# A gated cross-attention layer with routed experts: four row buffers, earlier W_qv loads, a split gather and a split last tile

## Chip, cores and metric

The kernel runs on one core of a Trainium2 chip. The metric is the device time of one execution in microseconds, median of several runs. Engines are called by their profile names: PE (TensorE matmul), PEld (its weight loads), DVE (VectorE), ACT (ScalarE), POOL (GpSimd), SP (SyncE, which here only issues DMAs).

## What is computed

Inputs are x (4096 x 512), a context of 3202 x 512, and the weights. Cut to what matters, the reference is:

```
# attention: queries = LN(x) = e, context = c
Sim  = (e @ w1)[:, None] + (c @ w2)[None, :] + (e * w3) @ c.T + b
hq   = softmax(Sim, axis=1) @ c
hc   = softmax(max(Sim, axis=1)) @ e                  # one row of 512
x    = x + tanh(g_x) * (concat[e, hq, e*hq, e*hc] @ W_qv + b_qv)     # W_qv: 2048 x 512
# routed feed-forward: 8 experts, top 2, CAP = 1.25 * 4096 / 8 = 640 rows each
xf   = LN(x); gates = softmax(xf @ w_router + b_router); top-2, kept while an expert has room
out  = gelu(rows_e @ w1[e] + b1[e]) @ w2[e] + b2[e]   # 512 -> 2048 -> 512 for each expert
x    = x + tanh(g_f) * (weighted sum of the kept outputs, divided by the kept weights' sum)
```

## The kernel before, in words

All matrix products are made of float16 pairs: an operand is split into a high and a low half, and three matmuls (high x high, high x low, low x high) add up in PSUM. One SBUF tensor, `arena`, is cut by hand into tiles for three stages which follow each other; each engine runs its own program and all order between them is by semaphores written out by hand.

**Attention** (`attention`) goes over 16 blocks of 256 rows, two units of 128 rows each, with the context in seven chunks of 512 (the last of 130). Each half of its loop does the scores of unit u on PE (line 1217), the exponentials of u-1 on ACT and DVE (lines 1048 to 1064 and 771), their transposes by DMA from SP (line 530) and the products of u-2 on PE (line 1233). Features (e, hq, e*hq as float16 pairs) go to DRAM (`store_f`, line 544). In the last two halves (`last=True`) no scores are left; SP loads the four parts of W_qv there (`load_weights`, line 266), ACT sums |W| part by part (`sum_part`, 276), POOL reduces over partitions (288), DVE makes the scales (297 to 309) and folds hc into the first part (`fold_part`, 339). Behind both halves ACT and DVE make the twelve high and low halves (`high` 359, `low` 373), and PE merges block 0 (`merge`, 367) once its features are back, transposed (`load_feats`, 249).

**Merge and routing** (`merge_and_route`) has blocks b = 0 to 15 of 256 rows. PE: 72 matmuls of 512 columns (line 1719, two row tiles q of twelve steps of three), and between them the counts of block b-2 (1752), the transposes of the rows of b-1 (1727) and the router of b-1 (1740). DVE, body b: second half of the routing of b-2 (`route_2`, 1513 to 1540), bias and matmul result added (1458, 1460), first half of the routing of b-1 (`route_1`, 1488 to 1504), the other row tile, then the norm (1468 to 1476) and the low halves (1480). ACT: copies of the transposed rows, the routing's exponential (1660), the square root (1662), the high halves (1667). The rows lie in `row[v]`, v = b % 2, a third one serving for the last block; POOL scatters them to the experts' lists in DRAM by four indirect DMAs per block (1426), waits until they have landed and then increments `row_free[v]` (1441), for which ACT and DVE of block b+2 wait. The first expert's w1 is prepared on the side: maxima on DVE (159) in blocks 6 to 9, scales behind 10, split by ACT and DVE (196, 202) in blocks 11 to 14. The last block goes row tile by row tile (`rows_last`, `norm_last`, `lows_last`, `route_1_last`, `route_2_last`).

**Experts** (`experts`), e = 0 to 7: rows of the expert gathered transposed (`turn_rows`, 1858, two DMAs of 320 rows), layer 1 in 16 feature tiles, each for two halves of 320 rows (2012), Gelu on ACT (1976), split on ACT and DVE (1979, 1935); layer 2 in five tiles of 128 rows (2027), whose result DVE scales and biases (1946), ACT weights (1992) and POOL adds to the output by an indirect DMA (1891).

Of the kernel before, what the change touches and what calls it, by code (L numbers as in the profile page):

```python
# [31 lines left out]
P = 128  # L32
# [174 lines left out]
class MergeOperands:  # L207
# [4 lines left out]
    def __init__(self, nc, st, arena, at, NB, w_qv, b_qv, g_x, g_f, w_r, b_r, hc):  # L212
# [12 lines left out]
        for v in range(2):  # L225
            self.ft[v] = take([3, 2, KD, 256], F16)
            self.x2[v] = take([2, D], F32)
            if v == 0:
                self.scores = off[0]
        self.end = off[0]  # L230
        take, _ = cutter(arena[:, at:])
# [32 lines left out]
    def load_weights(self, eng, n):  # L264
        part = slice(n * self.KD, (n + 1) * self.KD)
        eng.dma_start(self.W[:, part, :], self.w_qv.rearrange("(c p) d -> p c d", p=P)[:, part, :])\
           .then_inc(self.w_loaded[n], 16)

    def sum_part(self, act, n):
# [3 lines left out]
        if n:  # L273
# [3 lines left out]
                       self.W.rearrange("p c d -> p (c d)")[:, n * size:(n + 1) * size], ACT.Abs,  # L277
# [12 lines left out]
    def scales(self, dve):  # L290
# [4 lines left out]
        s.n = self.steps  # L295

# [29 lines left out]
    def fold_hc(self, dve):  # L326

        s = Steps(dve, self.prep, 0, 40)
        s.link(dve.reciprocal(self.rw, self.hc["wtot"]))
# [3 lines left out]
    def fold_part(self, dve, k):  # L333
# [5 lines left out]
        s.step(dve.scalar_tensor_tensor(out=self.W[:, k, :], in0=self.W[:, 3 * self.KD + k, :],  # L339
                                        scalar=self.hcn[:, k:k + 1], in1=self.W[:, k, :], op0=ALU.mult,  # L340
                                        op1=ALU.add))
        self.steps = s.n
# [14 lines left out]
    def high(self, act, k, ready):  # L357
        act.wait_ge(self.prep, ready)
        act.mul(self.Wt[:, k, 0, :], self.W[:, k, :], self.sc3[:, k // self.KD:k // self.KD + 1]).then_inc(self.w_hi, 1)

    def merge(self, pe, q, out):

        pe.wait_ge(self.f_loaded[0], 16)
        for k in range(self.FT):
            pe.wait_ge(self.w_lo, k + 1)
            for s, r in ((0, 0), (0, 1), (1, 0)):
                mm = pe.matmul(out[:, q, :], self.ft[0][:, k // self.KD, s, k % self.KD, q * P:(q + 1) * P],  # L367
                               self.Wt[:, k, r, :], start=(k + s + r == 0), stop=(k == self.FT - 1 and s == 1))
        mm.then_inc(self.y_done, 1)

    def low(self, dve, k):
        dve.wait_ge(self.w_hi, k + 1)
        dve.scalar_tensor_tensor(out=self.Wt[:, k, 1, :], in0=self.W[:, k, :],
# [4 lines left out]
def attention(nc, st, ps, arena, cst, x, ctx, w_sim, b_sim, feats, rows, hc_out, mg):  # L378
# [27 lines left out]
    qT = take([QT, 2 * KD, P], F16)  # L406
    qh = take([QT, 2, D], F16)
# [80 lines left out]
    COPIES = (0, 32, 64)  # L488
    UNIT0 = FIRST[0][LAST] + 1

# [6 lines left out]
    def sync(sp):  # L497
# [53 lines left out]
        def body(b, first=False, last=False, norms=True, loads=True, piece=None):  # L551
            u = 2 * b
            for c in range(NC):
# [14 lines left out]
                if c == 4 and not first:  # L568
                    store_f(u - 3, 1)
# [1548 lines left out]
```

## Time and profile before

| | |
|---|---|
| median of 3 runs (lowest, highest) | 2236.64 us (2236.12, 2238.46) |
| the profiled execution | 2254.05 us |
| its span, first to last instruction | 2252.3 us |
| PE busy | 96% of the span |
| DVE, ACT, POOL busy | 58%, 51%, 6% |
| mean granted clock of TensorE | 0.989 |

The shares are means over three stages with different limits, so they are read stage by stage: the timeline of an engine, the chain of waits, and the table of who waited for whom. Starts are in microseconds from the first instruction. Matmuls are pipelined: a row of the timeline ends about 0.16 us after the next one's start, so periods are taken from start to start.

### The profile page before, as it was taken

How to read it: one execution, taken by the hardware profiler on the slowest of the kernel's cores; microseconds unless marked ns; L12 is line 12 of the kernel's file. 1: busy time of each engine (PE TensorE's matmuls, PEld its weight loads, DVE VectorE, ACT ScalarE, POOL GpSimd, SP SyncE). 2: the span in 40 equal slices, each digit the busy share in tenths (PEclk: the TensorE clock that was granted, in tenths of full speed). 3: DMA queues.
4: the chain of work that ended last, by engine and by line, in shares of the span. 5: the costliest groups of instructions: out<-in, count | busy, mean ns of one | idle time of the engine just before them, and what ended most of it. 6: DMA issues, size and time to landing. Idle time of an engine off the chain costs nothing.

```text
span 2252.3 us, 34528 instructions
## 1 busy us (share of the span) xinstructions
PE 2172.4 (96%) x12015; PEld 1123.7 (50%) x12015; DVE 1301.3 (58%) x2712; ACT 1142.2 (51%) x1747; POOL 145.7 (6%) x141
## 2 busy tenths in 40 slices
PE   5999999999999999999999995999999999999997
PEld 2444444444444444444455442646565565647463
DVE  7756566655555665554667665555556464646450
ACT  6765565655555655655433342625354363636260
POOL 0000000000000000000022222010101010010101
PEclk9999999999999999999999997999999999999999
DMA  9534444444444444335987762353433333343511
GB/s 250 133 86 94 111 110 104 106 111 93 92 108 109 111 97 115 87 84 120 269 232 206 186 160 50 144 128 100 103 102 98 107 93 107 93 116 117 132 35 23
DMA packets 484566, 265.91 MB, mean 118 GB/s; under 512 B 423860, under 2 KB 423988, under 8 KB 480428
## 3 DMA queue, kind: packets, MB, share of 16 engines
q1 hardware_dynamic: 473644, 244.90, 41.6%
q0 software_dynamic: 10880, 20.52, 4.8%
q8 instruction: 18, 0.29, 0.1%
q14 instruction: 24, 0.20, 0.0%
HBM read 97.96 MB, written 71.52 MB: 75 GB/s over the span
## 4 chain that ended last, share of the span: by engine, by line
PE 88%; DMA 4%; DVE 4%; issue 2%; ACT 1%; POOL 1%; SPq 0%; POOLq 0%; DVEq 0%; ACTq 0%
PE ps L1217 23%; PE ps L1233 22%; PE ps L2012 19%; PE ps L2027 18%; PE ps L1719 5%; DMA rows<-arena 2%; PE ps L367 1%; POOL rows L1426 1%; DMA arena<-arena 1%; DMA arena<-in_ctx 1%; DVE arena L202 0%; DMA feats<-arena 0%; DVE arena L742 0%; DMA arena<-feats 0%; ACT arena L1667 0%
## 5 line engine op out<-in xcount | busy, mean ns | idle before, releaser
L1217 PE MATMUL ps<-arena 128*128 128x512 f16 (+1 forms) x2688 | 557.0, 358 | 4.8 <-DMA arena<-arena 3.1
L1233 PE MATMUL ps<-arena 128*128 128x512 f16 x2400 | 552.9, 379 | 0.0
L2012 PE MATMUL ps<-arena 128*128 128x320 f16 x3072 | 421.1, 300 | 12.2 <-DMA arena<-rows 12.2
L2027 PE MATMUL ps<-arena 128*128 128x512 f16 x1920 | 415.7, 379 | 0.0
L1217 PEld LDWEIGHTS ps<-arena 128*128 128x128 f16 x2688 | 250.1, 98 | 285.5 <-issue 4.9
L1233 PEld LDWEIGHTS ps<-arena 128*128 128x128 f16 x2400 | 233.6, 98 | 275.7
L2012 PEld LDWEIGHTS ps<-arena 128*128 128x128 f16 x3072 | 301.5, 98 | 131.5 <-DMA arena<-rows 12.2
L1038 ACT ACTIVATE arena<-ps,arena 128x512 f32<-128x512 f32 (+1 forms) x224 | 163.4, 731 | 389.6 <-PE ps L1217 389.5
L2027 PEld LDWEIGHTS ps<-arena 128*128 128x128 f16 x1920 | 187.9, 98 | 225.2
L758 DVE TENSOR_REDUCE arena<-arena 128x1 f32<-128x512 f32 (+1 forms) x224 | 139.9, 626 | 192.5 <-ACT arena L1038 191.7
L771 DVE SCALAR_TENSOR_TENSOR arena<-arena 128x512 f16<-128x512 f32 x192 | 144.1, 751 | 182.4 <-ACT arena L1059 182.4
L1719 PE MATMUL ps<-arena 128*128 128x512 f16 x1080 | 240.9, 380 | 0.0
L1935 DVE SCALAR_TENSOR_TENSOR arena<-arena 128x640 f16<-128x640 f32 x128 | 113.0, 883 | 133.9 <-ACT arena L1979 133.9
L196 ACT ACTIVATE arena<-arena 128x1024 f16<-128x1024 f32 x128 | 140.8, 1134 | 70.5 <-DVE arena L178 70.5
L202 DVE SCALAR_TENSOR_TENSOR arena<-arena 128x1024 f16<-128x1024 f32 x128 | 160.3, 1282 | 16.0 <-ACT arena L196 16.0
L1976 ACT ACTIVATE arena<-ps,arena 128x640 f32<-128x640 f32 x128 | 113.2, 885 | 107.6 <-PE ps L2012 107.5
L1059 ACT ACTIVATE arena<-arena 128x512 f16<-128x512 f32 x192 | 156.1, 813 | 21.4 <-DMA arena<-arena 8.2
L1719 PEld LDWEIGHTS ps<-arena 128*128 128x128 f16 x1080 | 103.0, 98 | 117.5 <-issue 1.8
L1946 DVE SCALAR_TENSOR_TENSOR arena<-ps,arena 128x512 f32<-128x512 f32 x40 | 30.0, 751 | 226.6 <-PE ps L2027 226.6
L1992 ACT ACTIVATE arena<-arena 128x512 f32<-128x512 f32 x40 | 28.8, 719 | 254.8 <-DVE arena L1946 252.9
L159 DVE TENSOR_REDUCE arena<-arena 128x1 f32<-128x2048 f32 x64 | 144.7, 2278 | 12.8 <-DMA arena<-in_L_ffn_w 12.8
L1048 ACT ACTIVATE arena<-arena 128x512 f32<-128x512 f32 (+1 forms) x224 | 149.1, 666 | 2.5 <-DVE arena L764 1.1
(245 smaller groups left out, 1380.3 us busy)
## 6 DMA issues: line engine op xcount, KB each, us to landing
arena<-in_L_ffn_w SPq DMA_DIRECT2D x64, 1024.0 KB, 10.2
feats<-arena SPq DMA_DIRECT2D x48, 512.0 KB, 2.8
arena<-in_x SPq DMA_DIRECT2D x32, 512.0 KB, 3.6
rows<-arena SPq DMA_DIRECT2D x13, 774.0 KB, 3.7
out<-arena SPq DMA_DIRECT2D x16, 512.0 KB, 3.0
arena<-in_ctx SPq DMA_DIRECT2D x6, 1024.0 KB, 13.4
arena<-arena SPq DMA_TRANSPOSE x276, 3.1
arena<-in_L_xattn_W_qv SPq DMA_DIRECT2D x4, 1024.0 KB, 7.9
```

The source lines that it names most:

```text
L159: s.step(dve.tensor_reduce(self.mw4[:, c:c + 1], self.raw[:, c * n:(c + 1) * n], AX.X, ALU.max, apply_absolute_value=True))
L196: act.mul(w[:, 0, c * n:(c + 1) * n], self.raw[:, c * n:(c + 1) * n], sc[:, 0:1]).then_inc(self.s_hi, 1)
L202: dve.scalar_tensor_tensor(out=w[:, 1, c * n:(c + 1) * n], in0=self.raw[:, c * n:(c + 1) * n], scalar=sc[:, 0:1], in1=w[:, 0, c * n:(c + 1 ...
L771: dve.scalar_tensor_tensor(out=stage[:, c % 2, 1, :], in0=p, scalar=pscale[:, c:c + 1], in1=stage[:, c % 2, 0, :], op0=ALU.mult, op1=ALU.s ...
L1038: act.activation(slot(par, c), psS[bank][:, 0:w], ACT.Identity, bias=zero[:, 0:1], scale=sinv[:, c:c + 1]).then_inc(scores_ready, 1)
L1048: act.activation(p, p, ACT.Exp, bias=neg[:, par:par + 1], accum_out=ls[:, par, c:c + 1])\
L1059: act.activation(stage[:, c % 2, 0, :], p, ACT.Identity, bias=zero[:, 0:1], scale=pscale[:, c:c + 1])\
L1217: mm = pe.matmul(out, qT[:, q, s * KD + k, :], ctxT[:, r * KD + k, a:z], start=(k == 0 and s + r == 0), stop=(k == KD - 1 and s == 1))
L1233: mm = pe.matmul(psO[q], turned, ctxN[:, j, r, :], start=(j + s + r == 0), stop=False)
L1719: mm = pe.matmul(psY[v][:, q, :], ft[v][:, k // KD, s, k % KD, q * P:(q + 1) * P], Wt[:, k, r, :], start=(k + s + r == 0), stop=(k == FT - ...
L2012: mm = pe.matmul(psH[:, f % 2, h, :], w1s[:, s, k * F + f * P:k * F + (f + 1) * P], XT[:, r, k, h * HALF:(h + 1) * HALF], start=(k + s + r ...
L2027: mm = pe.matmul(psO[:, t % 2, :], hT[:, f, s, t * P:(t + 1) * P], w2s[:, r, f * D:(f + 1) * D], start=(f + s + r == 0), stop=(f == KF - 1 ...
```

## The change

Four things are changed.

1. *W_qv and the features of block 0.* W is four tiles; the first two lie where the queries were and are loaded in the second half before the last two (`load_early`), the other two in the places of the first two loads. ACT sums them in chunks 0, 1, 4 and 5 of the half before last. The features of block 0 are requested in that half too (`load_first`). The twelve steps are taken in the order 4 to 11, 0 to 3, and the first five low halves are made before the fold.
2. *Merge and routing.* Four row buffers, b % 4; ACT and DVE wait for the scatter of b-4 directly, POOL for that of b-2, and `row_free` goes. The bias is added at the start of a body, bn_stats follows each row tile, and ACT makes the high half from x2 with scale and bias, no longer from DVE's normalised rows. The w1 maxima move to blocks 4 to 7, the scales behind 8, the split to 9 to 12. DVE, ACT and POOL run without loops. In the last block ACT's exponential of row tile 0 comes ahead of the square root of row tile 1.
3. *Experts.* Four gathers per expert: for each half of the rows first the high, then the low halves, with their own semaphores; layer 1 takes all matmuls of high rows first.
4. *The last tile of the last expert* is made in two halves of 256 columns, in other PSUM banks. ACT weights the bias beforehand, DVE makes the output in one operation per half, and POOL adds each half by a DMA of its own.

```diff
-        self.W = take([4 * KD, D], F32)
+        late = take([2 * KD, D], F32)
+        early = take([2 * KD, D], F32)
+        self.W = [early[:, 0:KD, :], early[:, KD:2 * KD, :], late[:, 0:KD, :], late[:, KD:2 * KD, :]]
+        self.ORDER = tuple(range(KD, FT)) + tuple(range(KD))
...
+        def load_early(n):
+            if n == 0:
+                for q in range(QT):
+                    sp.wait_ge(q_turned[q], 16 * (NB - 1))
+                sp.wait_ge(row_step, RK * U)
+                sp.wait_ge(e_out, 16 * NB)
+            mg.load_weights(sp, n)
...
-                if last and 1 <= c < 5:
+                if last and c in (1, 2):
                     if c == 1:
                         sp.wait_ge(qk_done, NC * U)
-                    mg.load_weights(sp, c - 1)
+                    mg.load_weights(sp, c + 1)
...
+                if last and c == 4:
+                    load_first()
...
+                if last and i and c == 1:
+                    mg.scales(dve)
+                    for n in range(AHEAD):
+                        mg.low(dve, n)
...
-                if last and not i and c >= 4:
-                    mg.sum_part(act, c - 4)
-                if last and i and c == 0:
-                    mg.sum_part(act, 3)
+                if last and not i and c in (0, 1, 4, 5):
+                    mg.sum_part(act, c if c < 2 else c - 2)
...
-    row = [take([QT, ROW], F32) for _ in range(3)]
+    row = [take([QT, ROW], F32) for _ in range(NR)]
...
+        for b in range(NB - 1):
+            pool.wait_ge(r_step, RK * (b + 1))
+            if b >= 2:
+                pool.wait_ge(sent[(b - 2) % NR], earlier(b - 2) + 16 * 2 * QT)
             for q in range(QT):
-                scatter(v, q, v)
+                scatter(b % NR, q)
+            if b == SCALED - 3:
+                ew.reduce_max(pool, 0)
...
             dve.wait_ge(y_done, QT * b + q + 1)
-            s.step(dve.scalar_tensor_tensor(out=x2[v][:, q, :], in0=(psY_first if first else psY[v])[:, q, :], scalar=cY[:, 0:1],
+            s.link(dve.scalar_tensor_tensor(out=x2[v][:, q, :], in0=(psY_first if first else psY[v])[:, q, :], scalar=cY[:, 0:1],
                                             in1=x2[v][:, q, :], op0=ALU.mult, op1=ALU.add))
+            s.step(dve.bn_stats(stats[:, q, :], x2[v][:, q, :]))
...
+            s.step(dve.scalar_tensor_tensor(out=shift, in0=mv[:, :, 0], scalar=-1.0, in1=rs, op0=ALU.mult, op1=ALU.mult))
...
+            if b >= NR:
+                act.wait_ge(sent[r], earlier(b))
+            act.wait_ge(y_step, YK * b + YN + 2)
+            for q in range(QT):
+                act.activation(halves[r][:, q, 0:D], x2[v][:, q, :], ACT.Identity, bias=shift[:, q:q + 1],
+                               scale=rs[:, q:q + 1]).then_inc(hi_done, 1)
...
+        for q in range(QT):
+            copy_turned(NB - 2, q)
+        sd_last(0)
+        exp_of(NB - 2)
+        high_last(0)
+        copy_turned(NB - 1, 0)
+        exp_last(0)
+        sd_last(1)
+        high_last(1)
+        copy_turned(NB - 1, 1)
+        exp_last(1)
...
             for h in range(2):
-                sp.dma_start_transpose(XT.rearrange("p s k c -> p (s k) c")[:, :, h * HALF:(h + 1) * HALF],
-                                       rows[bass.ds(e * CAP + h * HALF, HALF), 0:D].bitcast(F16))\
-                    .then_inc(xt_loaded[h], 16)
+                for r in range(2):
+                    sp.dma_start_transpose(XT[:, r, :, h * HALF:(h + 1) * HALF],
+                                           rows[bass.ds(e * CAP + h * HALF, HALF), r * D // 2:(r + 1) * D // 2].bitcast(F16))\
+                        .then_inc(xt_loaded[h][r], 16)
...
-                    for k in range(KD):
-                        for s, r in ((0, 0), (0, 1), (1, 0)):
+                    for s, r in ((0, 0), (1, 0), (0, 1)):
+                        if f == 0 and s == 0:
+                            pe.wait_ge(xt_loaded[h][r], 16 * (e + 1))
+                        for k in range(KD):
...
+        for c in range(2):
+            cols = slice(c * D // 2, (c + 1) * D // 2)
+            dve.wait_ge(o_done, ST * E + c)
+            dve.scalar_tensor_tensor(out=oa[TL % 2][:, cols], in0=psL[:, c, :], scalar=ali[:, TL:TL + 1],
+                                     in1=o32[TL % 2][:, cols], op0=ALU.mult, op1=ALU.add).then_inc(o_scaled, 1)
```

## Rows read from the trace of the kernel before

**Rows 1.** Busy time per engine in a stretch of merge blocks; PEclk, DMA share, GB/s last

```profile
1190.00:1225.00 35.00, 35.00 (x233) 17.54 (x232) 25.80 (x104) 13.69 (x18) 7.79 (x8) 1.00 0.72 205
```

**Rows 2.** The chain of waits in order of time: start, us, what

```profile
1259.33 9.09 DMA rows<-arena
...
1398.91 5.06 DMA arena<-rows
...
1510.65 52.16 PE ps L2012 x384
```

**Rows 3.** Who waited for whom, 1225 to 1362: total us, times, longest

```profile
ACT arena L1667 <- POOLq L1441: 29.5, 7, 7.3
...
PE ps L1727 <- DVE arena L1480: 8.2, 4, 3.7
```

**Rows 4.** Timeline of PE: start, us, engine, line, operation, count, [idle before]

```profile
1087.11 17.39 PE L367 MATMUL ps<-arena 128*128 128x512 f16 x72 [2.88 <-DMA arena<-feats]
...
1219.51 0.75 PE L1740 MATMUL ps<-arena 128*128 128x8 f16 x24
...
1244.97 0.17 PE L1752 MATMUL ps<-arena 128*128 128x16 f16 x1
...
1262.06 0.17 PE L1752 MATMUL ps<-arena 128*128 128x16 f16 x1
...
1357.54 0.17 PE L1752 MATMUL ps<-arena 128*128 128x16 f16 x1
```

**Rows 5.** Timeline of DVE and ACT behind the last merge matmul of a block

```profile
1225.37 0.75 DVE L1460 SCALAR_TENSOR_TENSOR arena<-ps,arena 128x512 f32<-128x512 f32 x1 [0.50 <-PE ps L1719]
...
1229.04 1.14 ACT L1667 CAST arena<-arena 128x512 f16<-128x512 f32 x2 [0.87 <-DVE arena L1476]
1229.69 1.29 DVE L1480 TENSOR_TENSOR arena<-arena 128x512 f16<-128x512 f32 x2 [0.28 <-ACT arena L1667]
```

**Rows 6.** Line 1059, ACT with scale and bias: ns min/median/max

```profile
L1059 ACT ACTIVATE arena<-arena x192: 812/812/816, 64.9 to 1069.4; 128x512 f16<-128x512 f32 x192
```

**Rows 7.** Timeline of DVE and ACT in the last block, 1362 to 1395

```profile
1363.18 2.48 DVE L202 SCALAR_TENSOR_TENSOR arena<-arena 128x1024 f16<-128x1024 f32 x2 [0.28 <-ACT arena L196]
...
1366.78 0.16 DVE L1513 TENSOR_REDUCE arena<-arena 128x2 f32<-128x16 f32 x1
...
1370.03 0.75 DVE L1575 SCALAR_TENSOR_TENSOR arena<-ps,arena 128x512 f32<-128x512 f32 x1
...
1373.70 0.15 DVE L1585 RECIPROCAL arena<-arena 128x1 f32<-128x1 f32 x1
...
1376.65 0.17 DVE L1513 TENSOR_REDUCE arena<-arena 128x2 f32<-128x16 f32 x1 [0.84 <-ACT arena L1689]
...
1383.73 0.17 DVE L1585 RECIPROCAL arena<-arena 128x1 f32<-128x1 f32 x1 [0.36 <-ACT arena L1675]
...
1385.33 1.28 ACT L1682 ACT_TABLE_LOAD   x1
...
1386.86 0.16 DVE L1513 TENSOR_REDUCE arena<-arena 128x1 f32<-128x8 f32 x1 [0.83 <-ACT arena L1682]
...
1394.34 0.22 DVE L1540 SCALAR_TENSOR_TENSOR arena<-arena 128x2 f32<-128x2 f32 x1
```

**Rows 8.** Timeline of all engines at the end of attention

```profile
1077.17 1.91 ACT L276 ACTIVATE arena<-arena 128x2048 f16<-128x2048 f32 x1 [1.61 <-DMA arena<-in_L_xattn_W_qv]
...
1078.57 6.35 SPq L249 DMA_TRANSPOSE arena<-feats  x1
...
1083.89 8.07 DVE L373 SCALAR_TENSOR_TENSOR arena<-arena 128x512 f16<-128x512 f32 x12 [0.79 <-ACT arena L359]
```

**Rows 9.** Line 530, probability transposes of 128 x 1024 float16, from issue

```profile
DMA to landing us min/median/max: 3.0/3.0/7.6
```

**Rows 10.** Timeline of all engines behind the last matmul, which ends at 2238.38

```profile
2238.48 0.75 DVE L1946 SCALAR_TENSOR_TENSOR arena<-ps,arena 128x512 f32<-128x512 f32 x1 [9.61 <-PE ps L2027]
...
2240.86 1.54 POOL L1891 DMA_INDIRECT out<-arena  x1 [8.81 <-ACT arena L1992]
```

More of the change, by code:

```diff
@@ L869, in half @@
                         total_weight()
-                    if c == 6:
+                    if c == 2:
                         mg.max_router(dve)
-                if last and i and c == 3:
-                    mg.scales(dve)
             if not (last and i):
@@ L989, in vector @@
             half(NB, i, last=True, norms=False)
-        for k in range(FT):
-            mg.low(dve, k)
+        for n in range(AHEAD, FT):
+            mg.low(dve, n)
         mg.router_scale(dve)
@@ L1172, in scalar @@
             half(NB, i, last=True, norms=False)
-        for k in range(FT):
-            mg.high(act, k, mg.scaled)
-            if k == 2:
+        for n in range(FT):
+            mg.high(act, n)
+            if n == 2:
                 mg.gates(act)
@@ L1345, in merge_and_route @@
     pk, kp, tot, away = (take([2, QT], F32) for _ in range(4))
-    dsti = [take([2, QT], U32) for _ in range(3)]
+    dsti = [take([2, QT], U32) for _ in range(NR)]
     wk, wsum, wi = take([QT, 2], F32), take([QT], F32), take([QT], F32)
@@ L1449, in gpsimd, with add_bias @@
         for q in range(QT):
             pool.wait_ge(r_step, RB + RQ * (q + 1))
-            scatter(2, q, 1)
+            scatter((NB - 1) % NR, q)
     def vector(dve):
+        def add_bias(b, v, q):
+            s = Steps(dve, y_step, b, YK)
+            s.n = q
+            s.step(dve.tensor_tensor(x2[v][:, q, :], x2[v][:, q, :], bqb, ALU.add))
         def y_part(b, v, q, first=False):
             s = Steps(dve, y_step, b, YK)
-            s.n = 2 * q
-            s.link(dve.tensor_tensor(x2[v][:, q, :], x2[v][:, q, :], bqb, ALU.add))
+            s.n = YQ[q] - 1
+            s.wait()
@@ L1464, in norm_part @@
+        def norm_part(b, v):
+            r = b % NR
             s = Steps(dve, y_step, b, YK)
-            s.n = 2 * QT
+            s.n = QT + 2 * QT
             s.wait()
-            for q in range(QT):
-                s.step(dve.bn_stats(stats[:, q, :], x2[v][:, q, :]))
-            s.wait()
-            apart(dve, dve_passed)
             for q in range(QT):
@@ L1864, in load_b2 @@
                 .then_inc(b2_loaded, 16)
[L1866 to L1867 removed]
+        for r in sent:
+            sp.wait_ge(r, 16 * rows_sent)
         turn_rows(0)
@@ L1887, in add_rows @@
         def add_rows(e, more=True):
-            for t in range(ST):
+            for t in range(ST if more else TL):
                 pool.wait_ge(o_scaled, ST * e + t + 1)
@@ L1938, in layer_2 @@
         def layer_2(e, more=True):
-            for t in range(ST):
+            for t in range(ST if more else TL):
                 n = e * ST + t
@@ L1983, in layer_2 @@
         def layer_2(e, more=True):
-            for t in range(ST):
+            for t in range(ST if more else TL):
                 n = e * ST + t
@@ L2030, in layer_2, with last_tile @@
                 mm.then_inc(o_done, 1)
-        with pe.Fori(0, E) as e:
+        def last_tile():
+            t = ST - 1
+            for c in range(2):
+                cols = slice(c * D // 2, (c + 1) * D // 2)
+                for f in range(KF):
+                    for s, r in ((0, 0), (0, 1), (1, 0)):
+                        mm = pe.matmul(psL[:, c, :], hT[:, f, s, t * P:(t + 1) * P],
+                                       w2s[:, r, f * D + cols.start:f * D + cols.stop],
+                                       start=(f + s + r == 0), stop=(f == KF - 1 and s == 1))
+                mm.then_inc(o_done, 1)
+        with pe.Fori(0, E - 1) as e:
             layer_1(e)
-            layer_2(e)
+            layer_2(e, ST)
+        layer_1(E - 1)
+        layer_2(E - 1, ST - 1)
+        last_tile()
     return sync, gpsimd, vector, scalar, tensor
```

360 lines of the change are left out of this document (173 added, 187 removed).

## The prediction

> **What bounds the kernel now.** I read the page first: TensorE (PE) is busy 96% of the span, so nearly every microsecond is a matmul slot, and only the places where PE stands can give time back. The chain of waits says where: attention runs PE-bound to 1084, the merge stage is PE-bound until about 1262, then the chain leaves PE, goes through the row scatters and VectorE (DVE), and returns to PE at 1404.0 for the experts, whose steady part has no gap [rows 2]. PE's own timeline gives the sizes. One merge block takes 17.09 us (1244.97 to 1262.06, same instruction), and the five blocks after it take 95.48 [rows 4]. Five periods, less 0.65 because the last block does its count one three-matmul step earlier, are 84.8: **10.7 us** are lost there. The table of waits names the holder: ScalarE's (ACT) high halves of the rows waited 29.5 us in 7 times for the POOL queue's line 1441, which frees a row buffer once its scatter has landed, and PE's transposes then waited for the low halves [rows 3]. One such scatter alone took 9.09 us [rows 2].
>
> **Part 1, four row buffers and the shorter row chain.** Block b now reuses the buffer of b-4, not of b-2, so the awaited scatter has two more periods, 34 us, against 9.09. What is late next? DVE. Its chain after the last merge matmul of a block runs from 1225.37 to the end of the low halves at 1230.98, 5.6 us [rows 5]; PE wants the rows 6.5 us after its block ends. The new chain has one bn_stats of 0.65 fewer behind the matmul, and ACT makes the high half beside the normalising DVE operation. That form of ACT operation (scale and bias per partition) costs 0.81 instead of 0.62 [rows 5, 6], so the chain comes to about 4.9. DVE's order over one block, each from the end of the previous merge: rows 4.9, then in the four blocks with w1 splitting until the second low part, 7.8 (two ACT pieces, two DVE pieces of 1.24 [rows 7]), two bias adds 9.2, second routing half 3.25 [rows 7] 12.4, first half row 13.9, first routing half 15.9. The matmul it waits for next ends at 17.09, so 1.2 us are left; in blocks with a maximum (2.28) more is left. In 35 us of such blocks DVE is busy 25.8 [rows 1]. Added DVE work is one tiny shift operation per block. Block 14 has two more bias adds (1.3) but no split behind it. I take all **10.7** back; bounds 6 (1.2 us late in each of four blocks) and 10.7. The loops written out and the removed semaphore increments I put at nothing, covered by the same slack.
>
> **Part 2, the end of the routing.** Count from T0, PE's start of the last block. Before, T0 is 1354.3 (the count at 1357.54, less five steps of 0.65) and DVE ends at 1394.56: 40.3 us [rows 4, 7]. It spent 12.5 us on rows that waited for a buffer, the last w1 split (2.48) and bias adds, before the routing of block 13 at 1366.78. New: rows until 4.9; routing of 13 until 8.1; wait for PE's first half (8.67: twelve steps of 0.65 and 0.9 of transposes) to 8.8; first half row 1.80, first routing of 14 1.9 (together 1370.03 to 1373.70 plus 0.05): 12.4. Normalise and low: 1.9, to 14.4. The exponential is ready by 12.4, so routing of 14 starts at once; before, it waited until 1376.65. From there to 1383.73 DVE ran without a hole, 7.1 us: 21.5. Normalise and low of the second half 1.85 (it was 3.13 up to 1386.86, where DVE waited for ACT's exponential behind a table load; that exponential is now ahead): 23.3. Then 7.7 as before (1386.86 to 1394.56): 31.1. PE is nearly ahead everywhere; its merge ends at 17.8, its last transposes and ACT's copy at 26.0, before DVE wants them at 26.3. Gain 40.3 - 31.1 = **9.2**; bounds 7 (an ACT table load lands on the chain, and PE is late once) and 10.
>
> A table load took 1.28 us here, and DVE had the activation's result 0.25 us behind its end [rows 7]; it starts ahead of the operands. The Trainium skill ("ScalarE: Activation LUTs", What ACT_TABLE_LOAD costs) speaks against this order: it gives 1.28 us plus a drain of 1.38, so 2.66 per switch. The new order puts the exponential's load ahead of the first high half; by that price the high half would be about 0.9 us late, and the part would give 8.3.
>
> **Part 3, the change of stage at 1084.** Before, PE stood 2.88 us for the feature transposes and ran a half-rate stretch, 17.39 us for 72 matmuls that take 15.55 at 216 ns [rows 4]. The transposes now start in the last attention half, so they are there. What is late next are the scaled weights. The last sum of |W| ended at 1079.2 because the fourth load landed at 1077.1 [rows 8]. With two loads already made a half earlier, the loads of the third and fourth part take the places of the first two, and ACT's order (two sums of 2.1 before the third probability chunk, two after the fifth and sixth) puts the last sum at about 1074.7, two chunks' transposes permitting; reduction 2.1, DVE's output row until 1078.6, scales 1.65: the first high half at 1080.3 instead of 1083.14. Twelve lows took 8.07, so 0.67 each [rows 8]: five until 1084.4. Then, new between them, DVE does totals, four folds and two output lows, 4.9: 1089.3; seven more lows end at 1094.0, and PE's first merge half ends one step later, 1094.7. Before it ended at 1087.11 + 17.39 - 7.77 (36 matmuls) = 1096.7. Gain **2.0**. Against: SyncE's queue (SP) issues the feature transposes in 6.35 us [rows 8], now ahead of the last two probability transposes of the last unit, and PE behind them. They would land at 1081.5 to 1083, where PE wants them at 1080.6 and 1083.2; up to 2.4 us of PE, mostly swallowed since DVE's lows are later. Bounds -1 (that, and a half-rate stretch again) and +4 (no DVE delay). The two early weight loads, one half before, compete with probability transposes that PE needs only a unit later: nothing.
>
> **Part 4, the first expert.** From the issue of the gather to PE's first matmul pass 5.06 us [rows 2]. That DMA moves 655 KB; the probability transposes of 262 KB land in 3.0 [rows 9]. A line through both gives 3.35 for a half of 327 KB: **1.7** earlier; the others follow at about 1.4 each while PE at half rate needs 2.1 us for each eight matmuls. Bounds 0 and 2.1. The other seven experts' gathers lie under layer 2 (240 matmuls of 216 ns, 51.8 us) and cost nothing. The Trainium skill ("DMA: Bandwidth & Descriptors", Anatomy of one DMA) has a fixed 2.0 us plus bytes / 436 GB/s, for the other kind of queue, and so speaks against halving; the rows' fixed part is about 1.6. By its figures a half would take 2.75, and the part would give 2.3.
>
> The new order of matmuls in layer 1 I put at nothing. All pitches here are columns / 2.4 GHz plus 2.5 ns: 52.16 us for 384 of 320 columns [rows 2]. Loads of weights hide even behind 8-column matmuls, 24 of which pass in 0.75 us [rows 4].
>
> **Part 5, the last tile.** Now DVE (0.75), ACT and an issue gap, then POOL's 1.54 at 2240.86 [rows 10]. New: one DVE operation of 256 columns, an estimated 0.50 (0.75 for 512 columns, 1.24 for 1024), and no ACT: 2.48 us from matmul to POOL become 1.45, a gain of 1.03. 96 matmuls of 256 columns take 109 ns each against 48 of 216: 0.1 lost. The first half's add is issued while the second is computed. Landing at the same 5 us: **0.9**; bounds 0 and 1.6 (half the bytes).
>
> **Sum:** 10.7 + 9.2 + 2.0 + 1.7 + 0.9 = 24.5. The profiled execution, 2254.05 (span 2252.3 and 1.75 around it), would become 2229.6. It is 17.4 above the median of the unprofiled runs, 2236.64; I carry the same gain over: **2212.1**.
>
> **Rivals.** (a) *DVE takes the scatter's place*: the 1.2 us of slack is not there, blocks with splits take about 18.2, and the tail keeps a late start: 10.7 becomes 6 and 9.2 becomes 7.5, time 2218.5. For: DVE's link-by-link waits; against: [rows 1]. Chance 0.18. (b) *The change of stage costs instead of gives*: PE waits for the last probability transposes behind the feature transposes and starts at half rate; part 3 is -1 to -2 and the time 2215.5. Chance 0.12. (c) *The profile itself swells the scatter*: without it the landings are shorter and half of the 10.7, and part of the late start, wasn't there to win: gain 16 to 18, time 2219.5. Chance 0.09. (d) *The buffers don't do what they say*: POOL now waits for the scatter of b-2 itself, and if that holds the sends, the rows come as late as before; 10.7 and some 3 of part 2 stay, time 2226. Against: that scatter has a full period. Chance 0.03. (e) *Slower*: layer 1 used each stationary tile twice in a row (high and low rows against the high weights); now never. If the second load of the same tile was free, each of 3072 matmuls pays; from 8 ns each (24.5 / 3072) the change loses, at 12 ns the time is 2249. Against: the router's 24 matmuls of 8 columns change their tile 16 times and take 31 ns each at most [rows 4], so a changed tile finds room beside 320 columns (133 ns). Chance 0.04; about 0.01 of it lies within 0.2% (some 7 to 9 ns).
>
> **How the numbers follow.** Forecast 0.54. Above, the range takes in rivals (a) to (c); below, parts 2 to 5 at their better ends give 2208, and 2 more are for the 17.4 us between profiled and unprofiled runs, which I can't place: 2206 to 2222. Some 0.2% (4.5 us) is what a measurement can tell from no change; only (e) reaches there. Faster 0.96, same 0.01, slower 0.03.
>
> **What would show it.** Merge blocks at 17.09 us without a hole until the last; no ACT wait for a buffer; from T0 to the last routing operation 31 us; the first merge half ending 2 us earlier; 3.4 us from the gather's issue to the first expert matmul; expert periods unchanged at 103.96; POOL's last issue 1.45 after the last matmul. Wrong would make it: PE waiting on DVE lows in blocks 9 to 13, layer 1 over 52.2 us, or a hole in the attention's last unit of more than 3 us.

## The result, and the profile after

The changed kernel takes **2230.61 us** (2229.95 to 2231.76, 8 runs), the kernel before in the same place 2237.84 us (2236.12 to 2241.26, 8 runs): ratio 0.9968, 95% interval 0.9959 to 0.9977. It is faster, by 7.2 us and not by 24.5: the forecast of 2212.1 and its range of 2206 to 2222 missed.

The profiled execution of the changed kernel took 2231.16 us (span 2229.4, clock 0.993). The prediction had 2229.6 for it, so the step from profiled to profiled execution came out within 1.6 us; the step from there to the median did not.

The timeline of PE in the changed kernel; columns as in [rows 4]:

```profile
1064.27 0.49 PE L1272 MATMUL ps<-identf,arena 128*128 128x128 f32 x2 [1.34 <-DVE arena L828]
1084.15 3.41 PE L1255 MATMUL ps<-arena 128*128 128x512 f16 x15 [1.96 <-DMA arena<-arena]
...
1124.59 0.17 PE L1766 MATMUL ps<-arena 128*128 128x16 f16 x1
...
1329.63 0.17 PE L1766 MATMUL ps<-arena 128*128 128x16 f16 x1
1346.07 0.17 PE L1766 MATMUL ps<-arena 128*128 128x16 f16 x1
...
1381.75 3.38 PE L2050 MATMUL ps<-arena 128*128 128x320 f16 x12 [10.55 <-DMA arena<-rows]
1385.46 11.94 PE L2050 MATMUL ps<-arena 128*128 128x320 f16 x84 [0.33 <-DMA arena<-rows]
1398.49 11.72 PE L2050 MATMUL ps<-arena 128*128 128x320 f16 x85 [1.09 <-ACT arena L2012]
```

Line 1766 is the count that was line 1752. Its first start is 1124.59, its thirteenth 1329.63: twelve periods of 17.09 us, and no row with a wait in brackets stands at the transposes of the rows between them. The fourteenth, at 1346.07, stands one step of three matmuls earlier in its block. In the old kernel's trace the same count stood at 1357.54 [rows 4].

DVE, SP and POOL at the end of the routing and of the kernel, and ACT's exponential ahead of the first high half of the last block, from the same timeline:

```profile
1353.86 1.28 ACT L1674 ACT_TABLE_LOAD   x1
1355.15 0.22 ACT L1674 ACTIVATE arena<-arena 128x20 f32<-128x20 f32 x1
1355.76 0.81 ACT L1702 ACTIVATE arena<-arena 128x512 f16<-128x512 f32 x1 [0.39 <-DVE arena L1606]
...
1373.69 0.22 DVE L1566 SCALAR_TENSOR_TENSOR arena<-arena 128x2 f32<-128x2 f32 x1
...
1378.27 6.12 SPq L1873 DMA_TRANSPOSE arena<-rows  x4
...
2217.46 0.48 DVE L2000 SCALAR_TENSOR_TENSOR arena<-ps,arena 128x256 f32<-128x256 f32 x1 [4.66 <-PE ps L2077]
2218.75 1.54 POOL L1923 DMA_INDIRECT out<-arena  x1 [2.25 <-DVE arena L2000]
```

These marks cut the kernel into five stretches, one for each part of the change. C1 and C14 are the first and the fourteenth count, R the end of DVE's last routing operation, Z the start of DVE's last operation on a matmul result, just behind the last matmul. All in us; "predicted" is the gain forecast for that stretch. The parts are numbered 1 to 5 as in the prediction, here and below: the last tile is part 5.

| stretch | before, profile | after, profile | gain | predicted |
|---|---|---|---|---|
| start to C1 (part 3) | 1125.37 | 1124.59 | 0.8 | 2.0 |
| C1 to C14 (part 1) | 232.17 | 221.48 | 10.7 | 10.7 |
| C14 to R (part 2) | 37.02 | 27.84 | 9.2 | 9.2 |
| R to Z (part 4) | 843.92 | 843.55 | 0.4 | 1.7 |
| Z to end (part 5) | 13.82 | 11.94 | 1.9 | 0.9 |
| span | 2252.3 | 2229.4 | 22.9 | 24.5 |

The two large terms are right to a tenth. And yet, of the 22.9 us between the two profiled spans, only 7.2 lie between the two medians. The question for the experiments is where the other 16 went.

### The profile page after: what moved, and what is told of

It is laid out like the page before. It is cut to its first block, busy times and chain, and to the rows that moved or that the text cites. A ratio compares the mean times of both kernels' runs of the same rounds, so it can differ in the third digit from the quotient of the medians.

```text
span 2229.4 us, 34453 instructions
## 1 busy us (share of the span) xinstructions
PE 2167.1 (97%) x12063; PEld 1125.5 (50%) x12063; DVE 1306.2 (59%) x2734; ACT 1148.8 (52%) x1747; POOL 144.9 (6%) x142
## 4 chain that ended last, share of the span: by engine, by line
PE 93%; DVE 2%; DMA 2%; ACT 1%; issue 1%; SPq 0%; POOL 0%; DVEq 0%; ACTq 0%; POOLq 0%
PE ps L1239 23%; PE ps L1255 22%; PE ps L2050 19%; PE ps L2065 18%; PE ps L1733 9%; DMA arena<-feats 1%; DMA arena<-arena 1%; DMA arena<-in_ctx 1%; PE ps L1741 1%; PE ps L2077 0%; DVE arena L764 0%; DVE arena L376 0%; PE ps L1754 0%; PE ps L1251 0%; ACT arena L278 0%
## 5 line engine op out<-in xcount | busy, mean ns | idle before, releaser
L159 DVE TENSOR_REDUCE arena<-arena 128x1 f32<-128x2048 f32 x64 | 144.7, 2279 | 12.2 <-DMA arena<-in_L_ffn_w 12.1
```

The source lines that it names most:

```text
L159: s.step(dve.tensor_reduce(self.mw4[:, c:c + 1], self.raw[:, c * n:(c + 1) * n], AX.X, ALU.max, apply_absolute_value=True))
```

## Experiments

The same kernels were run on several chips; B, C, D and E below are four different ones, in the order of use. Which one gave the result above isn't known.

### Chip B: the kernel before again, and three parts undone

**e1_before**: the kernel before, no edit. 

> The kernel before, unchanged, for a second trace of it. Theory T1 (the first trace is an odd execution): a new trace shows a span near 2236, its merge blocks lose about 0 to 3 us where the first lost 10.7, and ACT waits less than 10 us for row buffers. Theory T2 (the profiler swells the scatters): the new trace is again near 2252 with 10 us lost in blocks 10 to 14, while the executions beside it take 2238.

Measured: 2249.43 us over 10 runs, of which one with the profiler, as slow as the others (2249.61). Ratio to the other runs of the same kernel there 0.9993 (0.9983 to 1.0003). So the profiler doesn't swell the scatters, and the profiled execution on which the forecast rests wasn't an odd one either: on this chip every execution of the kernel before takes 2247 to 2257 us.

**e2_wait2**: the changed kernel, in which ACT and DVE wait for the scatter of block b-2 again, as with two buffers (the edit for ACT is shown; the same stands on DVE).

```
-            if b >= NR:
-                act.wait_ge(sent[r], earlier(b))
+            if b >= 2:
+                act.wait_ge(sent[(b - 2) % NR], earlier(b - 2) + 16 * 2 * QT)
```

> The changed kernel, but ACT and DVE wait for the scatter of block b-2 again, as with two buffers. T1: in a usual execution the scatter has landed by then, so at most 3 us slower than the changed kernel (2231 to 2234). T2, or the view that the scatter is the bound in every execution: 6 to 12 us slower (2237 to 2243).

Measured: 2261.09 us, 30 us over the next two kernels on the same chip, ratio to before 1.0041 (1.0026 to 1.0056). Its table of waits, 1120 to 1380 us:

```profile
ACT arena L1689 <- DMA rows<-arena: 51.6, 9, 7.5
DVE arena L1505 <- ACT arena L1689: 48.4, 9, 7.5
...
PE ps L1741 <- DVE arena L1505: 24.3, 7, 5.5
```

Both sizes I gave were too small. C1 to C14 took 254.46 us, 33 over the 221.48 of unhindered blocks. The wait feeds itself: rows that are late make the counts and the second routing half late, and with them the next scatter, for which the block after next waits. The kernel before, with the routing ahead of the bias adds, lost 6 to 14 us by the same wait (below). So on this chip the new order could not stand without the new buffers; e2 ran on no other.

**e3_wqv**: the changed kernel with part 3 undone, that is the loads of W_qv and of the features, the sums, the scales and the order of the twelve halves as before (the tiles' new places are kept). **e4_gather**: the changed kernel with part 4 undone, two gathers of 655 KB and layer 1 in the old order.

```
e3 -                if last and not i and c in (0, 1, 4, 5):
e3 -                    mg.sum_part(act, c if c < 2 else c - 2)
e3 +                if last and not i and c >= 4:
e3 +                    mg.sum_part(act, c - 4)
...
e4 -                for r in range(2):
e4 -                    sp.dma_start_transpose(XT[:, r, :, h * HALF:(h + 1) * HALF], ...
e4 +                sp.dma_start_transpose(XT.rearrange("p s k c -> p (s k) c")[:, :, h * HALF:(h + 1) * HALF], ...
```

> The changed kernel with the W_qv and feature loads, the sums, the scales and the order of the twelve steps as before, the tiles' new places kept. My part 3 gave 2.0 us: expected 2233. The trace of the changed kernel says otherwise: PE stood 2.0 and 1.3 us in attention's last unit and its first merge half ended at 1095.4 against 1096.7, a gain of 1.3, so 2232.

> The changed kernel with whole gathers and the old order of matmuls in layer 1. My part 4 gave 1.7 us: expected 2232.3. If the waits that the changed kernel's trace shows for the later quarters (0.3) and for ACT behind them (1.1) eat it, the time is 2230.5 to 2231.

Measured: 2230.77 us (ratio 0.9903, 0.9885 to 0.9920) and 2231.60 us (0.9909, 0.9893 to 0.9926). Both lie below what the prediction's terms gave, 2233 and 2232.3. The changed kernel itself wasn't run on chip B, so neither part can be told from nothing by its time. But both runs beat the kernel before by 18 to 20 us on this chip, where the result above shows 7: the changed kernel, less one part, stays at 2231, and it is the kernel before that moved.

### Chip C: what the kernel before waits for

**f1_before** and **f2_after**: the two kernels, no edit. **f3_before_half**: the kernel before with one scatter per row tile, and half the count in the waits for it. It leaves out the rows of the second choice, so its output is incomplete.

```
-            for k in range(2):
+            for k in range(1):
                 pool.indirect_dma_start(out=rows, ...
```

**f5_double**: the changed kernel with each scatter issued again, into a table that nothing reads.

```
-            for k in range(2):
+            for k, to in ((0, rows), (1, rows), (0, rows2), (1, rows2)):
                 pool.indirect_dma_start(out=to, ...
```

> The kernel before, unchanged, to be read beside the changed kernel on one chip. Theory T3: the landing of the row scatters (5 to 9 us each in the traces so far) differs from chip to chip, and the kernel before waits for it in the merge blocks. Then its median and the sum of what its merge blocks take over 17.09 us go together: near 2238 us with 0 to 4 us of such stalls, or near 2250 us with 10 to 16 us. Rival T4: the difference between chips is made elsewhere (change of stage, end, experts): the merge blocks of the trace lose 10 to 16 us whatever the median is.

> The changed kernel, unchanged. T3: 2231 us within 2 us on every chip, because nothing in its merge blocks waits for a scatter; all merge blocks 17.1 us. T4: it differs between chips as the kernel before does, so on a chip where that takes 2250 us this takes about 2243 us.

> The kernel before with the scatter of the first choice alone: that of the second choice is left out, so half of the routed rows never reach the row table and the output lacks them. Two scatters in place of four stand before each release of a row buffer. T3: the merge blocks take 17.1 us each and the time is 2233 to 2238 us on any chip, so 12 to 17 us under a before of 2250 us, and 0 to 4 us under a before of 2238 us. T4: within 3 us of the kernel before, save 1 to 2 us at the end of routing.

> The changed kernel with every row scatter issued a second time, into a second row table that nothing reads: eight scatters for a block in place of four. T3 with slack in the four buffers: merge blocks still 17.1 us, the end of routing 2 to 5 us later since the gathers wait for twice as many scatters: 2233 to 2236 us. Rival: four buffers only just cover it, the scatters' own issue or landing becomes the bound of a block, and the time rises by 10 to 40 us.

Measured: f1 2248.82 us (ratio 1.0002, 0.9989 to 1.0015), f2 2231.95 us (0.9922, 0.9902 to 0.9941), f3 2236.05 us (0.9939, 0.9920 to 0.9959), f5 2272.97 us (1.0107, 1.0087 to 1.0127). With half of its scatters the kernel before takes 13 us less, all its blocks take 17.09 us, and the time is within 2 us of what the whole kernel takes on the chip of the result (2237.84). The changed kernel is at 2232 here too. T3's times for f1, f2 and f3 hold; f1's profiled execution, the shortest of its runs (2245.11), lost 6.2 us in its blocks where I had written 10 to 16.

The time of f5 didn't come out. The busy time of the engines and, last, the DMA share and GB/s in two stretches of merge blocks, first of f5, then of the changed kernel of the result:

```profile
1140.00:1210.00 70.00, 64.17 (x430) 31.81 (x429) 47.71 (x185) 24.60 (x30) 27.16 (x28) 0.98 1.06 248
```

```profile
1140.00:1210.00 70.00, 70.00 (x465) 35.03 (x464) 51.27 (x203) 27.28 (x35) 15.56 (x16) 1.00 0.83 216
```

With twice the scatters the DMA share is 1.06 by the profile's count, against 0.83, POOL is busy 27 us against 16, and PE is busy 64 of 70 us. It isn't a buffer that is missing: neither ACT nor DVE waits for a scatter, but PE waits up to 5.41 us for transposed features, and C1 to C14 takes 238.70 us. Four buffers hide the landing of a scatter, not the transfers that it holds up; that these were held up by the load on the DMA engines is argued from the share, not shown by a run of its own.

### Chip D: the kernel before once more, and what is left in the changed one

**g0_before**: no edit. **g1_best**: the changed kernel with the sums of |W| one place later and the feature transposes of block 0 one chunk earlier.

```
-                if last and c == 4:
+                if last and c == 3:
                     load_first()
...
-                if last and not i and c in (0, 1, 4, 5):
-                    mg.sum_part(act, c if c < 2 else c - 2)
+                if last and not i and 2 <= c < 6:
+                    mg.sum_part(act, c - 2)
```

**g3_lasttile**: part 5 undone, `layer_2(E - 1, ST)` in place of `layer_2(E - 1, ST - 1)` and `last_tile()`, with what belongs to it on DVE, ACT and POOL. **g4_chain**: the four buffers kept, the row chain as before: the two `add_bias` behind `route_2_of`, and

```
-            act.wait_ge(y_step, YK * b + YN + 2)
             for q in range(QT):
-                act.activation(halves[r][:, q, 0:D], x2[v][:, q, :], ACT.Identity, bias=shift[:, q:q + 1],
-                               scale=rs[:, q:q + 1]).then_inc(hi_done, 1)
+                act.wait_ge(y_step, YK * b + YN + 3 + q)
+                act.copy(halves[r][:, q, 0:D], xn[:, q, :]).then_inc(hi_done, 1)
```

> The kernel before, unchanged, once more: on a chip where its median is near 2238 us, T3 (it waits there for scatters that land sooner) expects the merge blocks of the trace to lose 0 to 4 us over 17.09 us each; T4 (the difference lies elsewhere) expects 6 to 16 us as in the three traces so far. On a chip where its median is near 2250 us both expect 6 to 16 us.

> The changed kernel with the W_qv sums on ScalarE at chunks 2 to 5 in place of 0, 1, 4, 5, and the feature transposes of merge block 0 one chunk earlier on SP's queue. They aim at two holes of TensorE in the last attention unit of the changed kernel: 1.34 us at 1064.27 (pool row late behind the sums) and 1.96 us at 1084.15 (the transposes of the last two P chunks stand behind the feature transposes' issue of 7.28 us). Theory: both go, 3.3 us less, 2228.5 us. Rival: the sums at chunks 2 and 3 delay the probabilities instead, or the feature transposes hold back the P transposes of chunks 4 and 5: 2231 to 2234 us.

> The changed kernel with the last tile of the last expert undone: 48 matmuls of 512 columns, one bias step on DVE, one multiplication on ScalarE, one scatter-add. The prediction's step is worth 0.9 us, the two traces show 1.8 us (11.97 in place of 13.92 us behind the last matmul): 2232.4 us by the traces, 2231.5 us by the prediction. Rival: the landing of the last scatter-add is what differed between the traces by chance, and this takes 2230.6 to 2231 us.

> The changed kernel with its four row buffers, and the row chain in the blocks as before: the bias is added behind the second half of the routing, and ScalarE copies the high halves from the normalised rows in place of working them out from x2. Theory T3: the buffers alone keep the blocks free of waits: 17.1 us each, 2231 to 2232 us. Rival: the shorter chain is what keeps TensorE fed, and without it the transposes of the rows wait for DVE by 1 to 3 us in each of 13 blocks, 2240 to 2260 us.

Measured: g0 2250.49 us (ratio 1.0003, 0.9993 to 1.0013), g1 2228.07 us (0.9899, 0.9884 to 0.9914), g3 2234.49 us (0.9928, 0.9914 to 0.9941), g4 2229.91 us (0.9907, 0.9892 to 0.9922). The changed kernel itself wasn't run on chip D either. The old chain is no slower with four buffers: the blocks stay free without the shorter row chain. (g4 keeps the rest of part 1, the loops written out and the w1 work moved, so the buffers aren't tried quite alone.) g3 takes 13.87 us from Z to its end, as the kernel before does, so the last tile is worth its 1.9 us of the trace. g3 also has a wait of 2.99 us at the change of stage, where the changed kernel has 1.96, and the 15 matmuls behind it take 5.02 us in place of 3.41: the granted clock was 0.50 from 1084 to 1087, the lower of the two levels. g1 removes one hole, no wait stands at line 1272 any more, and of the transposes' 1.96 us this is left:

```profile
1078.49 1.69 PE L1255 MATMUL ps<-arena 128*128 128x512 f16 x7 [1.36 <-DMA arena<-arena]
```

### Chip E: the kernel before without its waits

**i_before** and **i_after**: the two kernels, no edit. **i_both**: g1 and g4 together. **i_c2**: as i_both, with `load_first()` at `c == 2`.

> The kernel before, unchanged, a fourth time. T3: if its median is near 2238 us here, its merge blocks lose 0 to 4 us over 17.09 us each; if it is near 2250 us, 6 to 16 us, as in the four traces so far. T4 (the difference between chips lies elsewhere): 6 to 16 us in both.

> The changed kernel, unchanged, for the two runs below to be read against: 2230.5 to 2232 us whatever the kernel before takes here (T3); 2242 us where that takes 2250 us, by T4.

> The changed kernel with two edits put together: the sums on ScalarE at chunks 2 to 5 and the feature transposes one chunk earlier (2228.1 us alone), and the row chain of the blocks as before, the bias behind the routing and the high halves copied from the normalised rows (2229.9 us alone). If the two gains are of different stretches they add: 2226 to 2227 us. Rival: the 1.3 to 2 us by which the old chain was faster are the spread between chips, and this takes 2228 us.

> As i_both, with the feature transposes two chunks earlier than in the changed kernel (chunk 2). In the trace with chunk 3 TensorE still waits 1.36 us at 1078.49 for P transposes. If these stand behind the feature transposes on SP's queue, one chunk more lifts it: 0.5 to 1.4 us less than i_both. Rival: the feature transposes then hold the P transposes of chunks 3 and 4 instead, and the time is 0 to 3 us more.

Measured: i_before 2238.28 us (ratio 0.9999, 0.9989 to 1.0008), i_after 2230.15 us (0.9964, 0.9951 to 0.9976), i_both 2227.71 us (0.9954, 0.9937 to 0.9971), i_c2 2234.61 us (0.9983, 0.9974 to 0.9993). This is a chip like that of the result, now with a trace of the kernel before. Its POOL and ACT around the four scatters of one block and the next use of the buffer:

```profile
1234.56 0.97 POOL L1426 DMA_INDIRECT rows<-arena  x1 [12.27 <-DVE arena L1540]
...
1238.40 0.98 POOL L1426 DMA_INDIRECT rows<-arena  x1 [0.30 <-issue]
...
1243.36 1.14 ACT L1667 CAST arena<-arena 128x512 f16<-128x512 f32 x2 [0.87 <-DVE arena L1476]
```

The same in g0, on chip D:

```profile
1236.51 0.97 POOL L1426 DMA_INDIRECT rows<-arena  x1 [12.97 <-DVE arena L1540]
...
1240.65 0.97 POOL L1426 DMA_INDIRECT rows<-arena  x1 [0.30 <-issue]
...
1248.83 1.14 ACT L1667 CAST arena<-arena 128x512 f16<-128x512 f32 x2 [6.00 <-POOLq L1441]
```

ACT wants the buffer 4.96 us after the last issue (1238.40 to 1243.36), in other blocks 4.4 to 7.3. On chip E it is free by then, and ACT waits for DVE alone, as in all blocks of that trace. On chip D it comes free only 8.2 us after the issue (1240.65 to 1248.83). The time from issue to landing (min, median, max) that the trace of chip E gives for these scatters, 1225 to 1350 us (in its earlier blocks it is 3.1, 4.3 and 5.5), and the waits for a buffer from 1225 to 1362 us on D, in f1 on C and in e1 on B (total, times, longest):

```profile
DMA to landing us min/median/max: 2.1/2.7/3.0
```

```profile
ACT arena L1667 <- POOLq L1441: 26.5, 5, 7.0
```

```profile
ACT arena L1667 <- POOLq L1441: 12.4, 3, 6.6
```

```profile
ACT arena L1667 <- POOLq L1441: 22.0, 5, 7.0
```

For i_before the table of waits has no such row. So what T3 says of the wait holds: whether the buffer is free when ACT wants it decides if the kernel before takes 2238 or 2250 us. What it says of the chips, that the scatters simply land later on some, was argued; the traces show something else beside every late landing. SP issues the transposes of a later block's features (line 249) at about the time of the last scatter. On chip E, then on chip D:

```profile
1239.78 6.46 SPq L249 DMA_TRANSPOSE arena<-feats  x1
```

```profile
1240.12 8.36 SPq L249 DMA_TRANSPOSE arena<-feats  x1
```

On E the last scatter (1238.40) is issued 1.38 us ahead of them, on D (1240.65) 0.53 us behind their start. In the five traces of the kernel before ACT waits 21 times for a buffer, and each time the last scatter was issued behind the start of SP's issue, by 0.03 to 1.79 us (17 times the transposes; in the last block that waits, 4 times, SP's store of line 1385). In the other 44 blocks it was issued ahead, by 0.36 to 3.73 us, and ACT never waits, on whatever chip: on chip C one that was 0.36 us ahead had landed within 3.9 us. f3 fits too: there the last scatter is 3.3 us ahead or more from 1218 us on. No run moves the one issue against the other, so this order is shown beside the waits and not yet as their cause.

The chips differ in when the scatters start. In the block above SP's issue starts 13.6 us behind PE's count on all of them, the first scatter 8.3 us behind it on E, but 9.4 to 10.0 on B, C, D and in the forecast's trace. It waits for DVE, and DVE there has waits that E has nowhere: before line 1488, which reads a matmul result, it stands 13.6 to 23.6 us in 3 to 6 times from 1120 to 1380 until something that the profile calls "remote". All traces of the changed kernel and its variants on B, C and D have such waits as well, those on E and of the result none. What it is, no record says. Each chip was used once, so a chip can't be told from its moment.

i_c2 shows the limit of moving SP's work forward. SP's queue, ACT and PE in its last attention half:

```profile
1061.23 11.02 SPq L251 DMA_TRANSPOSE arena<-feats  x1
...
1073.07 3.20 SPq L535 DMA_TRANSPOSE arena<-arena  x2
...
1077.39 0.81 ACT L1083 ACTIVATE arena<-arena 128x512 f16<-128x512 f32 x1 [8.43 <-DMA arena<-arena]
...
1079.11 1.23 PE L1276 MATMUL ps<-arena 128*128 128x1 f32 x5 [4.90 <-DVE arena L911]
```

The issue of the feature transposes blocks SP for 11 us here, the next probability transposes go out at 1073.07 (1064.17 in i_both), ACT waits 8.4 us and PE 4.9. The rival had the mechanism right and its size, 0 to 3 us, too small: 6.9 us more than i_both.

## Why the prediction was wrong, point by point

The stretches of the table above in all traces that bear on them (f3 and f5 have other scatters; e2 has other waits):

| kernel (chip) | start to C1 | C1 to C14 | C14 to R | R to Z | Z to end | median |
|---|---|---|---|---|---|---|
| before, forecast's trace | 1125.37 | 232.17 | 37.02 | 843.92 | 13.82 | 2236.64 |
| e1_before (B) | 1122.54 | 230.98 | 36.61 | 844.03 | 13.64 | 2249.43 |
| f1_before (C) | 1123.03 | 227.71 | 36.26 | 842.73 | 13.57 | 2248.82 |
| g0_before (D) | 1124.04 | 235.51 | 37.38 | 844.38 | 13.49 | 2250.49 |
| **i_before (E)** | 1123.70 | 221.48 | 34.31 | 843.12 | 13.89 | 2238.28 |
| after, result's trace | 1124.59 | 221.48 | 27.84 | 843.55 | 11.94 | 2230.61 |
| f2_after (C) | 1125.63 | 221.48 | 29.11 | 843.33 | 12.05 | 2231.95 |
| **i_after (E)** | 1123.55 | 221.48 | 27.85 | 843.03 | 11.99 | 2230.15 |
| e3_wqv (B) | 1125.44 | 221.48 | 29.31 | 842.67 | 12.00 | 2230.77 |
| e4_gather (B) | 1121.96 | 221.48 | 29.49 | 843.52 | 12.05 | 2231.60 |
| g1_best (D) | 1121.27 | 221.47 | 29.42 | 842.51 | 11.93 | 2228.07 |
| g3_lasttile (D) | 1125.65 | 221.48 | 29.46 | 842.54 | 13.87 | 2234.49 |
| g4_chain (D) | 1123.04 | 221.48 | 28.31 | 843.18 | 11.89 | 2229.91 |
| i_both (E) | 1121.68 | 221.48 | 27.81 | 842.53 | 11.90 | 2227.71 |
| i_c2 (E) | 1128.80 | 221.48 | 27.80 | 843.10 | 11.92 | 2234.61 |

- **What bounds the kernel now**: right for the trace it was read from, not for the runs it was to be compared with. The row of waits [rows 3], 2.6 to 7.3 us each, isn't in i_before at all.
- **Part 1**: the working was exact (10.7 against 10.7; 1.2 us of slack on DVE were enough) and the term is nothing on chip E, whose medians are those of the result: i_before and i_after both have 221.48.
- **Part 2**: 9.2 against the stalled trace, 6.5 on chip E (34.31 to 27.85), since 2.7 us of the old 37.0 were the same late buffer. On B, C and D the changed kernel and its variants need 28.3 to 29.5 here, on E and in the result 27.8. The steps hold: 27.84 and the 3.24 of five steps make 31.1 from T0. ACT's table load cost 1.28 us, and the exponential ran right behind it, 0.01 us later; the high half started at 1355.76 behind DVE. The Trainium skill ("ScalarE: Activation LUTs", What ACT_TABLE_LOAD costs) gives 2.66 us per switch; these rows don't bear it out.
- **Part 3**: predicted 2.0, measured 0. Traces with the old order (five of the kernel before, and e3) start C1 at 1124.0 on average, those with the new one (after, f2_after, i_after, e4, g3, g4) at 1124.1, each between 1122 and 1126. The wait ahead of the first merge, 1.6 to 3.0 us in the old order, is gone as forecast. The step that failed is the priced term "mostly swallowed": PE's last attention unit is not late behind the weights, so two new holes count in full, 1.34 us (the pool row, held by the sums on ACT, which had no price) and 1.96 us (P transposes behind the feature transposes' 7.28 us on SP's queue). All eight traces with the new order have the first at 1.33 or 1.34; the second is 0.34 in e4 and 2.99 in g3. g1 starts C1 at 1121.3. Nor was the 17.39 us stretch there to be won each time: e1, f1, g0 and i_before show the same 72 matmuls in 15.70 us.
- **Part 4**: predicted 1.7, measured 0.7 as a mean over the traces (843.6 for the six of the table with whole gathers, 842.9 for the nine with halves, which spread over 1.7 and 1.0). The first half did land early: issue 1378.27, PE 1381.75, 3.5 us, near the 3.35 of the line. The Trainium skill ("DMA: Bandwidth & Descriptors", Anatomy of one DMA) has figures for GpSimd's queue, from which the estimate was 2.75; this DMA of SP's took longer. PE then stood 0.33 us for a later part and 1.09 us for ACT's Gelu; that second wait I had not looked for.
- **Part 5**: predicted 0.9, the traces give 1.75 (13.71 to 11.96 on average), and g3 without it is 2.5 to 4.3 us over the three medians of the changed kernel, which wasn't itself run on chip D. The steps ahead of the DMA were right, 2217.46 to 2218.75; the term set at "landing at the same 5 us" was the wrong one. From POOL's last issue to the end pass 10.65 us with the split tile (2218.75 to 2229.4), 11.44 before and 11.5 in g3. The last issue moves half the bytes; that these are the reason isn't shown apart.
- **Sum and carry-over**: this is the step that failed. Span 2236.5 to 2227.9 on chip E is 8.6 us, of which 0.15, 0, 6.5, 0.1 and 1.9 in the table's five stretches. I wrote of the 17.4 us between the profiled execution and the median that I couldn't place them, and subtracted the whole gain from the median all the same. They can be placed: of the 15.8 us between the spans of the forecast's trace and of i_before, 10.7 lie in part 1's stretch, 2.7 in part 2's, 1.7 before C1 and 0.7 behind R. The median of 2236.64 never held what part 1 gives back, as far as a trace of another execution with the same time (i_before, 2238.22) can show it.
- **Rivals**: (c) had the right effect, a gain that isn't there to be won, with the wrong cause and under half the size; e1 excludes the profiler. (a), (d) and (e) aren't seen. Of (b), the wait for the last probability transposes is the second hole of part 3, and in f2 and g3 PE runs slower behind it as well. Layer 1 in its new order takes no longer (421 us of PE in all, before and after).

The two fastest versions are i_both, 2227.71 us, ratio 0.9954 to before where i_after has 0.9964, and g1_best, 2228.07. Against the changed kernel that is 2.4 us on chip E, where the two intervals overlap, so a gain isn't shown by time. C1 stands at 1121.7 against 1123.6, but e4, with the changed kernel's order up to there, has 1122.0 as well. What the traces do show is the first hole gone in both. The chain's order gives nothing that can be told; adding both gains was wrong.

## What to carry to other kernels

When the profiled execution is slower than the median, look first for a stall in it that hangs on a landing time with a small margin, and take the gap off that stall's gain before anything is carried over to the median. A ring of buffers that waits for a DMA with 5 us to spare made this kernel's time depend on the chip: on one the last DMA of a block was issued just ahead of another queue's large one, on others just behind. So look at what the other queues issue in the same two microseconds. Wherever the four buffers were used as such and the scatters not doubled, the time was 2228 to 2235 us, on all chips; the whole change is worth 17 us on chip C and 8 on chip E. Work moved ahead on a queue is paid by what stands behind it, so list that before moving a 7 us issue.

## What the runs showed of the hardware

- The same scatters land 2.1 to 3.0 us after their issue in one stretch of i_before, 3.1 to 5.5 in its earlier blocks; where the last of a block was issued behind the start of SP's next issue, ACT got its buffer 4.1 to 9.2 us after it (21 times in four traces of the kernel before). 2238 or 2250 us for the same kernel, while two sets of runs of it on one chip agree within 0.1% in their medians.
- The issue of one transposing DMA of the features occupied SP for 5.7 to 8.9 us in the merge blocks of all runs but f5 (up to 11.95 us), save the first one behind the change of stage, with 12.2 to 14.3 us, and for 11.02 us in attention's end of i_c2, while other traffic ran.
- A stretch of 72 matmuls right after the change of stage took 15.70 to 15.77 us in most traces, 17.39 us in two (the first of the kernel before, and e3_wqv) and 17.22 in f3. The granted clock from 1087 to 1104 us was 0.90 in the first of the kernel before, where PE had stood 2.88 us, and 1.00 in e1, where it had stood 2.37.
